# One core: an opening in which the norm of the first slot runs between two reaction pairs, and slot 0 has its own order

## The chip, the core and the metric

The kernel runs on one core of a Trainium2 chip. The metric is the device time of one execution in microseconds. The kernel before took 1431.0 us, the median of 3 runs (1430.63 to 1432.73). The engines are TensorE (PE), VectorE (DVE), ScalarE (ACT), GpSimd (POOL) and SyncE (SP), which here only issues transfers. Each has its own instruction queue, and they meet at semaphores alone.

## The reference

An input of 8 sequences of 256 tokens with 128 features runs through eight stages. The change touches the first two: a reaction-diffusion step, and four layers of a selective scan (Mamba). The later ones (an expert-routed feed-forward, a pooled attention, a quantized feed-forward) are unchanged. Cut to what matters:

```python
def cond(y, zX, zY, zR):                       # the "reaction"
    lap_x = y[.., :-2] - 2*y + y[.., 2:]       # along the features (reflected ends)
    lap_y = y[:-2] - 2*y + y[2:]               # along the tokens
    return zX*lap_x + zY*lap_y + zR*y*(1 - y)

for i in range(4):                             # layers
    x = x + mamba(layer_norm(x, ln_g, ln_b), ...)
# mamba: in-projection; causal convolution of 4 taps; silu; xdbl = x_proj(xm)
#   dt = softplus(dt_w @ xdbl[:8] + dt_b); B, C = the other 32 rows of xdbl
#   h[t] = exp(dt*A) * h[t-1] + dt*B*xm        # 16 states for each of 256 channels
#   y = sum_s h*C + xm*D_skip; y *= silu(z); out-projection
```

## The kernel before, in words

Features lie on the 128 partitions. The 8 sequences are taken in **pairs** (512 columns), and a pair in one layer is a **slot**: 16 slots, numbered by t; slot t handles pair t mod 4 in layer t div 4. In a slot the two sequences are called a and b. The scan over time runs in 8 chunks of 2 states for each sequence: chunk c of sequence a needs `dA:ac` (ScalarE, four exponentials into PSUM, L1198), `mul:ac` (the product of B and u, L1214 on VectorE or L1220 on GpSimd), `scan:ac` (VectorE, L1233), `C:ac` (product with C, GpSimd, L1239) and `sum:ac` (TensorE, L1268). `gate:a` (VectorE, L1277) follows the last sum.

While a slot scans, the engines prepare the next slot's front: `center` (TensorE L1060, x minus its mean), `square` (ScalarE L1064), `var` (TensorE L1068), `lnv` and `rstd` (ScalarE L1072, L1076), `norm` (VectorE L1080), `xn` (ScalarE L1085), `conv` (TensorE L1093, 16 matmuls), `xm` (L1100), `z` and `zs` (L1106, L1112), `xproj` (L1119), `xd` (L1126), `dt` (TensorE L1130, ScalarE L1144 to L1152, VectorE L1156) and `u` (L1164, half on VectorE and half on GpSimd). `ucopy` (ScalarE L1182) copies u into PSUM for VectorE's products. SP writes xd to memory (L995) and spreads its rows over all partitions: B0 and B1 (tile Bb), C0 and C1 (tile Cb), 2 MB each (L1001).

The order on each engine in a slot is a string of such names (`PE_ORDER`, `ACT_ORDER`, `DVE_ORDER`, `POOL_ORDER`), which `in_order` turns into code; a leading `l` means the previous slot's b, `n` the next slot's a, and `+` the slot after the next. Slot 0 and slot 13 are written out, slots 1 to 12 are a loop of two slots a pass, and slots 14 and 15 have orders of their own with the next stage woven in. In slot 0 the names of a previous slot are left out.

Ahead of slot 0 is the **opening**. TensorE turns the input (L1796, four turns of 4 transposes) and takes the laplacian along the features (L1803); ScalarE copies (L1831, L1838); GpSimd computes the product `rate(k)` of pair k (L1758) and, for each layer L, `bundle(L)`: one product of the in-projection with the taps (L1768) and two diagonal matrices (L1772). VectorE's `reaction(k)` has eight instructions (L1880 to L1890) and ends with pair k in `xs`. The bundles of layers 1 to 3 are stored in memory by SP (`store`, L975). The first convolution needs bundle 0 and the norm of pair 0, which needs `reaction(0)`. The first products overwrite what the reactions use, so they wait for all four reactions, and those of sequence b for the three stores.

Of the kernel before, what the change touches and what calls it, by code (L numbers as in the profile page):

```python
# [15 lines left out]
B, S, D = 8, 256, 128  # L16
# [70 lines left out]
def program(nc, io):  # L87
    with ExitStack() as ctx:
# [869 lines left out]
        def _(e):  # L958
# [65 lines left out]
            store(1)  # L1024
            e.wait_ge(sem("scr"), 16)
            raw(3)
            store(2)
            store(3)
            e.wait_ge(sem("scr"), 16 * (LAYERS - 1))
            for k, n in enumerate(("itok_B_0_7", "itok_B_0_2")):  # L1030
                e.dma_start(ids[:, k * B:(k + 1) * B], io[n].rearrange("(a b) -> a b", a=1)).then_inc(sem("ids_in"), 16)
            for t in range(SLOTS):
                L, r = divmod(t, NPAIR)
                if r == 1 and L:
                    load_out(L)
# [677 lines left out]
            for token in order.split():  # L1713
                piece(e, table, token, -1, 1)

        def slots(e, slot):

            slot(e, 0, 0, False, 2)
            with e.Fori(0, (SLOTS - 4) // 2) as j:
                slot(e, j * 2 + 1, 1, True, 2)  # L1720
                slot(e, j * 2 + 2, 0, True, 2)
            slot(e, SLOTS - 3, (SLOTS - 3) % 2, True, 2)
# [3 lines left out]
        def _(e):  # L1726
# [64 lines left out]
        @block.tensor  # L1791
        def _(e):

            def turn(k):
                for j in range(4):
                    m = e.transpose(bank(k)[:, j * P:(j + 1) * P], xtok[:, 4 * k + j, :], ident[:])  # L1796
                m.then_inc(sem("xT_ps"), 1)

            def lap(k):
                e.wait_ge(sem("xT"), TURNED[k])  # L1800
                if k > 1:
                    e.wait_ge(sem("xT"), TURNED[k - 2])
# [12 lines left out]
            first(e, PE, "center var")
            lap(2)
            lap(3)
            first(e, PE, "conv:0 conv:1 z:0 z:1 xproj dt:0 dt:1 +center +var")
            slots(e, in_order(PE, PE_ORDER))
            last(e, PE, FINAL_PE, PE_NEXT, LAST - 1)  # L1820
            last(e, PE, FINAL_PE, PE_LAST)
            tail_tensor(e)
# [4 lines left out]
        @block.scalar  # L1827
        def _(e):
            def turned(k):
                e.wait_ge(sem("xT_ps"), TURNED[k])  # L1830
                e.activation(ypad[:, 2 * k:2 * k + 2, 1:S + 1], bank(k).rearrange("p (b l) -> p b l", b=2),  # L1831
                             ACT.Copy).then_inc(sem("xT"), 1)

            def lap(k):
                e.wait_ge(sem("xT_ps"), LAPPED[k])
                e.wait_ge(sem("z_in"), 48)
                for b in range(2):
                    m = e.activation(lapx[:, 2 * k + b, :], bank((4 + k) % 6)[:, b * S:(b + 1) * S], ACT.Identity,  # L1838
                                     scale=zb[:, 0, 2 * k + b:2 * k + b + 1])
# [12 lines left out]
            e.wait_ge(sem("A"), 1)  # L1852
            e.activation(A_all[:], A_all[:], ACT.Copy, scale=-1.0).then_inc(sem("A"), 1)
            first(e, ACTE, "silus")
            lap(2)
            lap(3)
            e.wait_ge(sem("A"), 2)
            first(e, ACTE, "xm:0 xm:1 zs:0 zs:1 exps xd sp_abs sp_exp sp_ln ucopy:n dA:n0 dA:n1 +square +lnv +rstd")
            slots(e, in_order(ACTE, ACT_ORDER))
            last(e, ACTE, FINAL_ACT, ACT_NEXT, LAST - 1)  # L1860
            last(e, ACTE, FINAL_ACT, ACT_LAST)
            tail_scalar(e)
# [5 lines left out]
        def _(e):  # L1868
# [4 lines left out]
                ins.then_inc(sem("du"), 1)  # L1873
                e.wait_ge(sem("du"), count[0])

            def reaction(k):
                bb = slice(2 * k, 2 * k + 2)
                y, lx, ly, g = ypad[:, bb, 1:S + 1], lapx[:, bb, :], lapy[:, bb, :], grow[:, bb, :]
                e.wait_ge(sem("xT"), TURNED[k])
                du(e.tensor_copy(ypad[:, bb, 0:1], ypad[:, bb, 2:3]))  # L1880
                du(e.tensor_copy(ypad[:, bb, S + 1:S + 2], ypad[:, bb, S - 1:S]))
# [1 line left out]
                du(e.scalar_tensor_tensor(out=ly, in0=y, scalar=-2.0, in1=ly, op0=ALU.mult, op1=ALU.add))  # L1883
                e.wait_ge(sem("z_in"), 48)
                du(e.tensor_tensor(ly, ly, zb[:, 1, bb].unsqueeze(2).to_broadcast([P, 2, S]), ALU.mult))
                e.wait_ge(sem("rise"), k + 1)
                du(e.scalar_tensor_tensor(out=g, in0=y, scalar=-1.0, in1=rise[:, bb, :], op0=ALU.add, op1=ALU.mult))
                du(e.tensor_tensor(g, ly, g, ALU.subtract))
# [150 lines left out]
```

## Time and profile before

| | |
|---|---|
| median of 3 runs | 1431.0 us |
| profiled execution | 1420.1 us, span 1418.3 us |
| mean granted TensorE clock | 0.961 |
| busy: PE, DVE, ACT, POOL | 90%, 82%, 71%, 79% |
| first product of slot 0 (DVE L1214) | 50.61 us |
| first product of slot 1 | 106.34 us |
| first and last norm (L1080) among the slots | 58.03 and 774.05 us |

The norm that stands in slot t belongs to the front of slot t + 1; the norm of slot 0's own front is that in the opening, at 25.87 us. The shares are averages over a kernel with several stages: up to about 890 us the scan runs, and VectorE and GpSimd are the fullest engines; afterwards it is other work. All times in the rows are from the start of the span. A number in square brackets behind a row is the time in which the engine was idle before it, with what ended that.

### The profile page before, as it was taken

To read this page: it belongs to the slowest core of one execution; us is meant where nothing else is said; L and a number is where in the kernel's file an instruction comes from. 1 tells how busy PE (TensorE), PEld (TensorE's weight loads), DVE (VectorE), ACT (ScalarE), POOL (GpSimd) and SP (SyncE) were. 2 spreads that over 40 slices of the span, in tenths; PEclk is the share of its full clock that TensorE was granted. 3 is DMA by queue.
4 is the path that set the end of the run, shared out by engine and by line. 5 is a ranking of instruction groups with operands and counts; after the bars stand their busy time and mean duration, and the time that the engine had idled before them with its cause. 6 is when DMAs were issued, how large, how long until landed. Compare 5 with 4: busy or idle time off the path is not lost.

```text
span 1418.3 us, 19878 instructions
## 1 busy us (share of the span) xinstructions
PE 1273.4 (90%) x5370; PEld 708.4 (50%) x5379; DVE 1164.4 (82%) x1686; ACT 1010.6 (71%) x2389; POOL 1116.7 (79%) x684
## 2 busy tenths in 40 slices
PE   5689899898998999989989999879959999999994
PEld 2233443343443334334333355679945666766663
DVE  7599999999999999999999989755644576666664
ACT  3588788778878878878877887433326787887773
POOL 7499999999999999999999997044444777766662
PEclk8799999999999999999999999989978999999997
DMA  5541543443355254254345361413220000000000
GB/s 170 239 180 62 237 200 124 181 179 157 140 207 214 83 238 179 74 244 179 139 167 222 135 196 64 149 37 104 65 64 17 7 22 24 12 20 17 9 9 9
DMA packets 48978, 169.26 MB, mean 119 GB/s; under 512 B 15704, under 2 KB 33436, under 8 KB 40716
## 3 DMA queue, kind: packets, MB, share of 16 engines
q1 hardware_dynamic: 46636, 163.78, 30.1%
q0 software_dynamic: 2272, 4.66, 1.4%
q8 instruction: 31, 0.51, 0.1%
q14 instruction: 39, 0.32, 0.1%
HBM read 160.75 MB, written 7.67 MB: 119 GB/s over the span
## 4 chain that ended last, share of the span: by engine, by line
PE 46%; DVE 24%; ACT 14%; issue 11%; POOL 2%; DMA 2%; DVEq 0%; ACTq 0%; POOLq 0%; SPq 0%
DVE h L1233 13%; ACT banks L1198 10%; PE banks L1268 7%; DVE h L1214 5%; PE banks L403 5%; PE banks L728 3%; PE banks L789 3%; PE banks L766 3%; PE banks L412 2%; PE banks L670 2%; PE banks L685 2%; PE banks L1119 2%; PE banks L705 2%; PE banks L804 2%; PE banks L1285 2%
## 5 line engine op out<-in xcount | busy, mean ns | idle before, releaser
L1239 POOL TENSOR_TENSOR h<-h,Cb 128x1024 f32<-128x1024 f32 (+1 forms) x180 | 584.5, 3275 | 29.7 <-DVE h L1233 18.6
L1233 DVE TENSOR_TENSOR_SCAN h<-banks,h 128x1024 f32<-128x1024 f32 x256 | 573.9, 2278 | 15.7 <-ACT banks L1198 15.4
L1198 ACT ACTIVATE banks<-dt,A_cur 128x255 f32<-128x255 f32 x1024 | 422.4, 461 | 89.0 <-DVE h L1233 86.8
L1268 PE MATMUL banks<-h,ident 128*128 128x512 f32 x1024 | 468.9, 597 | 5.2 <-POOL h L1239 3.3
L1268 PEld LDWEIGHTS banks<-h,ident 128*128 128x128 f32 x1024 | 189.8, 190 | 248.8 <-issue 225.9
L1214 DVE TENSOR_TENSOR h<-Bb,banks 128x1024 f32<-128x1024 f32 (+1 forms) x131 | 204.7, 1568 | 2.9 <-ACT banks L1182 2.9
L1220 POOL TENSOR_TENSOR h<-Bb,u 128x1024 f32<-128x1024 f32 x80 | 188.6, 2369 | 0.3 <-DMA Bb<-scrX 0.3
L758 POOL TENSOR_SCALAR h<-h 128x128 f32<-128x128 f32 (+1 forms) x128 | 96.3, 768 | 59.5 <-DVE h L751 59.3
L758 POOL TENSOR_SCALAR Cb<-Cb,h 128x128 f32<-128x128 f32 (+1 forms) x128 | 102.6, 819 | 32.5 <-DVE h L751 32.4
L1093 PE MATMUL banks<-xn,wF 128*128 128x512 f32 x256 | 117.6, 612 | 8.8 <-ACT xn L1085 8.8
L1093 PEld LDWEIGHTS banks<-xn,wF 128*128 128x128 f32 x256 | 49.8, 196 | 75.1 <-issue 63.1
L403 PE MATMUL banks<-Cb 128*128 128x128 f32 x624 | 78.2, 280 | 0.0
L382 POOL COPY Bb<-Bb 128x1 int32 x39 | 10.5, 269 | 85.0 <-DVE Bb L1637 45.4
L403 PEld LDWEIGHTS banks<-Cb 128*128 128x128 f32 x624 | 75.0, 197 | 0.0
L737 DVE CUSTOM_DVE_ANT_0 h<-banks,Bb 128x128 f32<-128x128 f32 (+1 forms) x128 | 39.1, 352 | 30.0 <-PE banks L728 29.5
L728 PE MATMUL banks<-h 64*128 64x128 f32 (+1 forms) x512 | 59.3, 350 | 0.5 <-DVE h L737 0.4
L488 DVE TENSOR_TENSOR Cb<-Cb,banks 128x512 f32<-128x512 f32 x39 | 26.8, 688 | 37.9 <-PE banks L403 37.9
L745 ACT ACTIVATE h<-h 128x128 f32<-128x128 f32 (+1 forms) x128 | 56.7, 450 | 0.0
L745 ACT ACTIVATE Cb<-Cb,h 128x128 f32<-128x128 f32 (+1 forms) x128 | 56.5, 446 | 0.1
L789 PE MATMUL banks<-Bb,h 128*64 128x256 f32 (+1 forms) x512 | 55.8, 338 | 0.3 <-issue 0.3
L737 DVE CUSTOM_DVE_ANT_0 Cb<-banks,Bb 128x128 f32<-128x128 f32 (+1 forms) x128 | 39.2, 352 | 17.0 <-PE banks L728 16.2
L451 ACT ACTIVATE Cb<-banks 128x128 f32<-128x128 f32 x39 | 10.8, 278 | 56.2 <-PE banks L395 56.2
(295 smaller groups left out, 2047.3 us busy)
## 6 DMA issues: line engine op xcount, KB each, us to landing
Bb<-scrX SPq DMA_DIRECT2D x32, 2048.0 KB, 8.1
Cb<-scrX SPq DMA_DIRECT2D x32, 2048.0 KB, 9.6
h<-in_L_ffn_w SPq DMA_DIRECT2D x2, 2048.0 KB, 8.7
by_expert<-Cb SPq DMA_DIRECT2D x39, 64.0 KB, 1.5
h<-in_conv_w SPq DMA_DIRECT2D x4, 512.0 KB, 3.9
scr<-h SPq DMA_DIRECT2D x3, 640.0 KB, 3.0
wF<-scr SPq DMA_DIRECT2D x3, 512.0 KB
dt<-in_pmask SPq DMA_DIRECT2D x4, 257.0 KB, 2.7
```

Source lines behind the costliest of these rows:

```text
L403: m = e.matmul(bank(2 * w + q)[:, c * P:(c + 1) * P], w_now[q][w][:, c * P:(c + 1) * P], xgT[k], start=True, stop=True)
L728: m = e.matmul(bank(o)[:, lo:lo + n], qT[r:r + HS, p, jc * P:(jc + 1) * P], kT[r:r + HS, p, 0:n], start=True, stop=True)
L745: m = e.activation(Pr[h % 8][:, lo:lo + n], Pr[h % 8][:, lo:lo + n], ACT.Exp, bias=negm[:, jc, h:h + 1], scale=-1.0, accum_out=sums[:, jc, ...
L758: m = e.tensor_scalar(Pr[h % 8][:, lo:lo + n], Pr[h % 8][:, lo:lo + n], inv[:, jc, h:h + 1], None, ALU.mult)
L789: m = e.matmul(bank(4, S)[o * HS:(o + 1) * HS, q0:q0 + n], V[:, kc, h * HS:(h + 1) * HS], PT[h % 4][:, 2 * P * kc:2 * P * kc + n], start=( ...
L1093: m = e.matmul(ps_F[half][:].rearrange("p (b l) -> p b l", b=2), wF[:, FC_TAP + k * 2 * P + half * P:FC_TAP + k * 2 * P + (half + 1) * P], ...
L1198: m = e.activation(ps_dA[c % 2][:, g, half, 1:S], dts[q][:, half, i * S + 1:(i + 1) * S], ACT.Exp, scale=A_cur[q][:, s:s + 1])
L1214: e.tensor_tensor(h[i][:, rows(cs), :, :], both(Bb[i], cs), u_rows(ps_u, cs), ALU.mult).then_inc(sem("mulv"), len(cs))
L1220: e.tensor_tensor(h[i][:, rows(cs), :, :], both(Bb[i], cs), u_rows(us[q][:, :, i * S:(i + 1) * S], cs), ALU.mult).then_inc(sem("mulp"), le ...
L1233: e.tensor_tensor_scan(chunk(i, c), ps_dA_flat[c % 2], chunk(i, c), 0.0, ALU.mult, ALU.add).then_inc(sem("scan"), 1)
L1239: e.tensor_tensor(h[i][:, rows(cs), :, :], h[i][:, rows(cs), :, :], both(Cb[i], cs), ALU.mult).then_inc(sem("hC"), len(cs))
L1268: m = e.matmul(bank(5), ident[:], h_flat[i][:, s * HALVES * S:(s + 1) * HALVES * S], start=(s == 0), stop=(s == NS - 1))
```

## The change

Five edits. (1) In the opening GpSimd waits for `reaction(0)` before `bundle(0)`, and its order becomes rate 0, bundle 0, rate 1, bundle 1, rate 2, rate 3, bundle 2, bundle 3. (2) VectorE's reaction is cut in two: `across(k)`, the first five instructions, and `reaction(k)`, the last three; the norm now stands between `across(1)` and `reaction(1)`. (3) SP issues stores 2 and 3 after B0 and C0 of slot 0 instead of ahead of slot 0, and no longer waits there for the stores to land. (4) ScalarE and VectorE have an order of their own for slot 0 (`ACT_OPEN`, `DVE_OPEN`); GpSimd and TensorE keep theirs. (5) ahead of slot 0 ScalarE runs `+square` before `dA:n1` instead of after it.

```diff
@@ SP
             raw(3)
-            store(2)
-            store(3)
-            e.wait_ge(sem("scr"), 16 * (LAYERS - 1))
...
                 spread_B(t, 0)
                 spread_C(t, 0)
+                if t == 0:
+                    store(2)
+                    store(3)
                 spread_B(t, 1)
@@ every engine
-        def slots(e, slot):
-            slot(e, 0, 0, False, 2)
+        def slots(e, slot, opening):
+            opening(e, 0, 0, False, 2)
@@ GpSimd
             rate(0)
+            e.wait_ge(sem("res"), 1)
             bundle(0)
+            rate(1)
             bundle(1)
-            rate(1)
             rate(2)
+            rate(3)
             bundle(2)
-            rate(3)
             bundle(3)
@@ ScalarE
-            first(e, ACTE, "xm:0 ... ucopy:n dA:n0 dA:n1 +square +lnv +rstd")
+            first(e, ACTE, "xm:0 ... ucopy:n dA:n0 +square dA:n1 +lnv +rstd")
@@ VectorE
+            across(0)
             reaction(0)
-            reaction(1)
+            across(1)
             e.wait_ge(sem("ln_in"), 32)
             first(e, DVE, "norm")
-            reaction(2)
-            reaction(3)
+            reaction(1)
+            for k in (2, 3):
+                across(k)
+                reaction(k)
@@ the order of slot 0 on VectorE, first line
+mul:a0 scan:a0 mul:a12 scan:a1 norm scan:a2 mul:a4 scan:a3 scan:a4 gate:l mul:a6 scan:a5 scan:a6 mul:b0 scan:a7
```

VectorE in the opening. Before, the last three instructions of reaction 1 (L1887 to L1890) stand ahead of the norm (L1080):

```order
L1882 TENSOR_TENSOR h0<-ypad 128x512
L1883 SCALAR_TENSOR_TENSOR h0<-ypad,h0 128x512
L1885 TENSOR_TENSOR h0<-h0,zb 128x512
L1887 SCALAR_TENSOR_TENSOR h0<-ypad,h0 128x512
L1888 TENSOR_TENSOR h0<-h0 128x512
L1890 TENSOR_TENSOR xs<-h0 128x512
L1080 SCALAR_TENSOR_TENSOR xc<-banks,lng,rstd 128x512
```

and in the changed kernel, where they are L1892 to L1895:

```order
L1883 TENSOR_TENSOR h0<-ypad 128x512
L1884 SCALAR_TENSOR_TENSOR h0<-ypad,h0 128x512
L1886 TENSOR_TENSOR h0<-h0,zb 128x512
L1080 SCALAR_TENSOR_TENSOR xc<-banks,lng,rstd 128x512
L1892 SCALAR_TENSOR_TENSOR h0<-ypad,h0 128x512
L1893 TENSOR_TENSOR h0<-h0 128x512
L1895 TENSOR_TENSOR xs<-h0 128x512
```

The norm moved up past three instructions. VectorE at the start of slot 0, before (L1214 is a product, of two chunks where it is 2048 wide; L1233 a scan of one chunk):

```order
L1164 TENSOR_TENSOR u0<-dt0,xm0 128x512
L1214 TENSOR_TENSOR h0<-Bb0,banks 128x2048
L1080 SCALAR_TENSOR_TENSOR xc<-banks,lng,rstd 128x512
L1233 SCALAR_TENSOR_TENSOR h0<-banks,h0 128x1024
L1214 TENSOR_TENSOR h0<-Bb0,banks 128x1024
L1233 SCALAR_TENSOR_TENSOR h0<-banks,h0 128x1024 x2
```

and now:

```order
L1164 TENSOR_TENSOR u0<-dt0,xm0 128x512
L1214 TENSOR_TENSOR h0<-Bb0,banks 128x1024
L1233 SCALAR_TENSOR_TENSOR h0<-banks,h0 128x1024
L1214 TENSOR_TENSOR h0<-Bb0,banks 128x2048
L1233 SCALAR_TENSOR_TENSOR h0<-banks,h0 128x1024
L1080 SCALAR_TENSOR_TENSOR xc<-banks,lng,rstd 128x512
L1233 SCALAR_TENSOR_TENSOR h0<-banks,h0 128x1024
```

Two scans now stand ahead of the norm. ScalarE from the copy of u (L1182) ahead of slot 0, before (x4 of L1198 is one dA chunk):

```order
L1182 ACTIVATE banks<-u 128x512
L1188 ACTIVATE A_cur<-A_all 128x32
L1198 ACTIVATE banks<-dt,A_cur 128x255 x8
L1064 ACTIVATE rstd<-banks 128x512
L1072 ACTIVATE rstd<-banks,eps 128x512
L1076 ACTIVATE rstd<-rstd 128x512
L1085 ACTIVATE xn<-xc,lnb 128x2x256
L1198 ACTIVATE banks<-dt,A_cur 128x255 x12
L1134 ACT_TABLE_LOAD
L1100 ACTIVATE xm<-banks,wF 128x512 x2
```

and now:

```order
L1188 ACTIVATE A_cur<-A_all 128x32
L1198 ACTIVATE banks<-dt,A_cur 128x255 x4
L1064 ACTIVATE rstd<-banks 128x512
L1198 ACTIVATE banks<-dt,A_cur 128x255 x4
L1072 ACTIVATE rstd<-banks,eps 128x512
L1076 ACTIVATE rstd<-rstd 128x512
L1198 ACTIVATE banks<-dt,A_cur 128x255 x4
L1085 ACTIVATE xn<-xc,lnb 128x2x256
L1198 ACTIVATE banks<-dt,A_cur 128x255 x16
L1134 ACT_TABLE_LOAD
L1100 ACTIVATE xm<-banks,wF 128x512 x2
```

One dA chunk now stands behind the square, one ahead of xn, and four (a3 to a6) instead of three (a2 to a4) between xn and xm.

## Rows read from the trace of the kernel before

**Rows 1.** Busy time by stretch: start:end, length, each engine (instructions), PEclk, DMA share, GB/s

```profile
25.00:30.00 5.00, 2.58 (x3) 1.18 (x4) 4.90 (x6) 3.30 (x7) 5.00 (x5) 0.50 0.40 153
...
50.60:106.30 55.70, 43.81 (x89) 17.51 (x90) 49.81 (x27) 43.74 (x89) 45.08 (x16) 0.84 0.53 218
...
315.00:368.00 53.00, 49.22 (x113) 20.82 (x112) 51.15 (x29) 41.62 (x84) 50.78 (x18) 0.97 0.39 160
368.00:420.00 52.00, 48.30 (x115) 20.55 (x114) 51.65 (x30) 42.27 (x86) 51.54 (x19) 1.00 0.44 176
```

**Rows 2.** Timeline of DVE in the opening: start us, us, instruction, [idle before]

```profile
7.89 0.17 DVE L1880 COPY ypad<-ypad 128x2 f32<-128x2 f32 x1 [7.74 <-ACT ypad L1831]
...
11.19 2.72 DVE L1887 SCALAR_TENSOR_TENSOR h<-ypad,h 128x512 f32<-128x512 f32 x1
13.95 0.74 DVE L1888 TENSOR_TENSOR h<-h 128x512 f32<-128x512 f32 x1
...
25.87 0.74 DVE L1080 SCALAR_TENSOR_TENSOR xc<-banks,lng,rstd 128x512 f32<-128x512 f32 x1
...
34.21 0.16 DVE L1880 COPY ypad<-ypad 128x2 f32<-128x2 f32 x1
...
38.24 0.69 DVE L1890 TENSOR_TENSOR xs<-h 128x512 f32<-128x512 f32 x1
...
46.82 1.22 DVE L1156 SCALAR_TENSOR_TENSOR dt<-banks,sp 128x1024 f32<-128x1024 f32 x1 [7.81 <-ACT sp L1152]
```

**Rows 3.** Timeline of POOL in the opening

```profile
10.49 2.88 POOL L1768 TENSOR_TENSOR wF<-h 128x1024 f32<-128x1024 f32 x1 [1.53 <-DMA h<-in_skip]
13.35 1.81 POOL L1772 TENSOR_SCALAR wS<-ident,h 128x128 f32<-128x128 f32 x2
...
19.20 2.68 POOL L1758 TENSOR_TENSOR h<-ypad,zb 128x512 f32<-128x512 f32 x2
```

**Rows 4.** Timeline of PE in the opening, and the convolution of slot 1

```profile
13.72 0.78 PE L1796 MATMUL banks<-ident,h 128*128 128x128 f32 x4
15.52 1.12 PE L1060 MATMUL banks<-xs,center_w 128*128 128x512 f32 x2 [1.02 <-DVE xs L1890]
...
27.42 8.97 PE L1093 MATMUL banks<-xn,wF 128*128 128x512 f32 x16 [5.54 <-ACT xn L1085]
...
110.79 7.03 PE L1093 MATMUL banks<-xn,wF 128*128 128x512 f32 x16
```

**Rows 5.** Timeline of ACT in the opening

```profile
20.04 0.63 ACT L1076 ACTIVATE rstd<-rstd 128x512 f32<-128x512 f32 x1
```

**Rows 6.** Timeline of DVE at the start of slot 0

```profile
50.61 2.29 DVE L1214 TENSOR_TENSOR h<-Bb,banks 128x2048 f32<-128x2048 f32 x1 [1.84 <-ACT banks L1182]
58.03 0.75 DVE L1080 SCALAR_TENSOR_TENSOR xc<-banks,lng,rstd 128x512 f32<-128x512 f32 x1 [5.13 <-ACT rstd L1076]
58.69 2.28 DVE L1233 TENSOR_TENSOR_SCAN h<-banks,h 128x1024 f32<-128x1024 f32 x1
```

**Rows 7.** Timeline of ACT at the start of slot 0: two dA chunks

```profile
50.70 3.26 ACT L1198 ACTIVATE banks<-dt,A_cur 128x255 f32<-128x255 f32 x8
```

**Rows 8.** Timeline of POOL in slot 0: C:a01 and C:a2

```profile
64.42 6.84 POOL L1239 TENSOR_TENSOR h<-h,Cb 128x2048 f32<-128x2048 f32 x2 [7.23 <-DVE h L1233]
```

**Rows 9.** Transfers into Bb from 40 to 70 us: B0 is the shortest, B1 the longest

```profile
L1001 SPq DMA_DIRECT2D Bb<-scrX x2: 350/392/433, 43.2 to 44.0; - x2
...
DMA to landing us min/median/max: 6.9/11.5/16.2
```

**Rows 10.** Timeline of PE in the loop, the gap before L1283

```profile
327.96 1.97 PE L1283 MATMUL banks<-xs,ident 128*128 x2 [2.05 <-DVE yz L1277]
```

**Rows 11.** Timeline of DVE: three norms of the loop

```profile
313.17 0.75 DVE L1080 SCALAR_TENSOR_TENSOR xc<-banks,lng,rstd 128x512 f32<-128x512 f32 x1
365.67 0.74 DVE L1080 SCALAR_TENSOR_TENSOR xc<-banks,lng,rstd 128x512 f32<-128x512 f32 x1
416.36 0.75 DVE L1080 SCALAR_TENSOR_TENSOR xc<-banks,lng,rstd 128x512 f32<-128x512 f32 x1
```

More of the change, by code:

```diff
@@ L1775, in _ @@
             rate(0)
+            e.wait_ge(sem("res"), 1)
             bundle(0)
+            rate(1)
             bundle(1)
-            rate(1)
             rate(2)
+            rate(3)
             bundle(2)
-            rate(3)
             bundle(3)
             first(e, POOL, "u:0")
-            slots(e, in_order(POOL, POOL_ORDER))
+            slots(e, in_order(POOL, POOL_ORDER), in_order(POOL, POOL_ORDER))
             last(e, POOL, {}, POOL_NEXT, LAST - 1)
@@ L1818, in _ @@
             first(e, PE, "conv:0 conv:1 z:0 z:1 xproj dt:0 dt:1 +center +var")
-            slots(e, in_order(PE, PE_ORDER))
+            slots(e, in_order(PE, PE_ORDER), in_order(PE, PE_ORDER))
             last(e, PE, FINAL_PE, PE_NEXT, LAST - 1)
@@ L1857, in _ @@
             e.wait_ge(sem("A"), 2)
-            first(e, ACTE, "xm:0 xm:1 zs:0 zs:1 exps xd sp_abs sp_exp sp_ln ucopy:n dA:n0 dA:n1 +square +lnv +rstd")
-            slots(e, in_order(ACTE, ACT_ORDER))
+            first(e, ACTE, "xm:0 xm:1 zs:0 zs:1 exps xd sp_abs sp_exp sp_ln ucopy:n dA:n0 +square dA:n1 +lnv +rstd")
+            slots(e, in_order(ACTE, ACT_ORDER), in_order(ACTE, ACT_OPEN))
             last(e, ACTE, FINAL_ACT, ACT_NEXT, LAST - 1)
@@ L1874, in du, with across @@
                 e.wait_ge(sem("du"), count[0])
-            def reaction(k):
+            def across(k):
                 bb = slice(2 * k, 2 * k + 2)
-                y, lx, ly, g = ypad[:, bb, 1:S + 1], lapx[:, bb, :], lapy[:, bb, :], grow[:, bb, :]
+                y, ly = ypad[:, bb, 1:S + 1], lapy[:, bb, :]
                 e.wait_ge(sem("xT"), TURNED[k])
@@ L1885, in reaction @@
                 du(e.tensor_tensor(ly, ly, zb[:, 1, bb].unsqueeze(2).to_broadcast([P, 2, S]), ALU.mult))
+            def reaction(k):
+                bb = slice(2 * k, 2 * k + 2)
+                y, lx, ly, g = ypad[:, bb, 1:S + 1], lapx[:, bb, :], lapy[:, bb, :], grow[:, bb, :]
                 e.wait_ge(sem("rise"), k + 1)
@@ L1903, in _ @@
             first(e, DVE, "dt u:1")
-            slots(e, in_order(DVE, DVE_ORDER))
+            slots(e, in_order(DVE, DVE_ORDER), in_order(DVE, DVE_OPEN))
             r = Chain(e, "du", count[0])
@@ L1941 @@
 mul:a3 mul:a5 C:l7 mul:a7 C:a01 C:a2 mul:b3 C:a34 mul:b6 C:a56 C:a7 C:b0 C:b12 C:b3 u C:b4 C:b56"""
+ACT_OPEN = """
+dA:a2 xn dA:a3 dA:a4 dA:a5 dA:a6 silus xm:0 xm:1 exps ucopy:b dA:a7 dA:b0 silus zs:0 zs:1 exps dA:b1 xd dA:b2
+dA:b3 sp_abs sp_exp sp_ln dA:b4 dA:b5 +square dA:b6 dA:b7 +lnv +rstd ucopy:n dA:n0 dA:n1"""
+DVE_OPEN = """
+mul:a0 scan:a0 mul:a12 scan:a1 norm scan:a2 mul:a4 scan:a3 scan:a4 gate:l mul:a6 scan:a5 scan:a6 mul:b0 scan:a7
+mul:b12 scan:b0 scan:b1 scan:b2 mul:b45 scan:b3 mul:b7 dt gate:a scan:b4 scan:b5 scan:b6 scan:b7"""
 PE_NEXT = """
```

## The prediction, made before the changed kernel ran

> **What bounds the kernel now.** I read the busy time of stretches first, then the timelines of the opening engine by engine, then slot 0, then the starts of the norms in the loop. In the loop VectorE and GpSimd are full: in 368 to 420 us VectorE works 51.65 of 52 us and GpSimd 51.54 [rows 1]. What the change touches lies ahead of that. Slot 0 (50.6 to 106.3 us) has VectorE busy for 49.81 of 55.70 us, so 5.9 us are idle there, and 5.13 us of it stand in one place, ahead of the second norm [rows 1, 6]. Before slot 0 the path runs: first turn, reaction of pair 0 on VectorE, center and variance on TensorE, rstd on ScalarE, **norm** on VectorE, xn, 16 convolution matmuls, xm, z, xproj, xd, dt, u, first product at 50.61. Two things are slack on that path. rstd is ready at 20.67, but the norm starts at 25.87 because the reaction of pair 1 stands ahead of it in VectorE's queue [rows 2, 5]. And VectorE's short operations are stretched while GpSimd runs two-input products: L1887 takes 2.72 us beside the first bundle (10.49 to 13.37) where L1890, of the same shape and also with two inputs from SBUF, takes 0.69 once GpSimd is silent (38.24) [rows 2, 3]. The two alternate: each waits until the other's instruction is over.
>
> The whole stay of VectorE from 7.89 to 38.93 us is 31.0 us; the last reaction, run alone, takes 34.21 to 38.93, 4.72 us. Four of them and the norm are 19.6, so 11.4 us were waited. GpSimd's own two-input work is 4 bundles at about 2.2 (2.88 less the 0.69 that it waited itself) and 4 rates at about 0.65 (2.68 for two, half of it waiting), 11.4 us as well [rows 2, 3]. VectorE waits for all of it.
>
> **Part 1, bundles behind the first reaction.** Bundle 0 now starts after xs of pair 0. L1887 loses 2.03 us (2.72 to 0.69), so xs ends at 13.44 instead of 15.47. The rate ahead of it is unmoved. TensorE can use only part of that: its fourth turn runs 13.72 to 14.50, and center, which began at 15.52, can begin at 14.52 [rows 4]. Gain 1.00 us; rstd, which ended at 20.67 [rows 5], ends at 19.67.
>
> **Part 2, norm ahead of the rest of reaction 1.** After 13.44 VectorE has five instructions (across 1) before the norm. Alone they are 2 x 0.17 + 3 x 0.72 = 2.5 us, by the reaction that ran alone [rows 2]; bundle 0's product (2.2) and rate 1 (0.65, beside one of them) are waited for, which ends them at about 18.5. So rstd decides, the norm starts at 19.7, and the gain at the norm is 25.87 - 19.7 = 6.2 us. Bounds: 5.2 if TensorE gains nothing at center, 7.4 if rstd gains more than center does and VectorE's own 18.5 decides.
>
> **Part 3, the convolution's clock.** The 16 matmuls take 8.97 us here and 7.03 in slot 1 [rows 4]. The mean granted clock from 25 to 30 us was 0.50 (1.2 GHz) [rows 1], and TensorE had sat idle 5.54 us before the convolution. Its work ahead of that (the laps) ended at 21.9; now it ends near 20 and the convolution starts at 21.2, one or two us later. The saving lies between 0 and 1.94; I take 1.4, nearer the short gap. Parts 1 to 3: **7.6 us** at xd and dt, the conv-to-xd stretch being unchanged. B's transfer starts from xd and so moves with it: it landed 6.9 us after its issue, just before the first product [rows 9].
>
> **Part 4, what becomes late next.** Moving work behind the norm makes VectorE's reactions 1 to 3 the thing to watch, for dt (46.82 before, now wanted at 39.2) stands behind them. From 7.89: 18.9 us of reactions, 0.75 of norm, rate 0 (0.75), and the GpSimd products that fall on VectorE's work. Bundle 1's product runs mostly while VectorE waits for rstd (1.1 us) or norms from PSUM, which GpSimd does not hold up. The rest is 2.05 + 0.5 + 0.35 + 2 x 0.65 + 2 x 2.2 = 8.6. End: 7.89 + 18.9 + 0.75 + 0.75 + 8.6 + 1.1 = 38.0. That is 1.2 us ahead of dt. With every product on VectorE (11.4) it is 39.9, and the gain at dt falls to 6.9; at best the gain there is capped at 8.8. GpSimd ends its bundles near 33, far ahead of u. On SP, raw 2 and raw 3 follow bundle 0 and store 1 by some 2 to 3 us more than before, and have that time.
>
> **Part 5, stores 2 and 3 moved past B0 and C0.** They no longer stand between bundle 3 and scrX, whose xd now comes at about 33.4 us. They stand ahead of B1 and C1 instead: 1.28 MB at some 400 GB/s are 3.3 us. B1 landed 16.2 us after its issue at 44.0 [rows 9], T + 9.6 (T is the first product, 50.6 before); now T + 12.9. GpSimd's mul:b3, its first user, comes at T + 15.2 in part 6. Cost 0, with 2.3 us of cover; beyond it the cost would be what GpSimd cannot absorb.
>
> **Part 6, slot 0.** Before: product a01, then VectorE idle until rstd at T + 7.4, norm, scan a0 from T + 8.1 although its dA was ready at T + 1.8 [rows 6, 7]. Now, with 1.65 us for a dA chunk (half of 3.26), 2.2 for a scan, 1.1 and 2.2 for products: scan a0 1.8 to 4.0, product a12 to 6.2, scan a1 to 8.4, norm to 9.1, scan a2 to 11.3, product a4, scan a3 from 12.4, where before it began at T + 16.9: 4.5 us gained. ScalarE runs dA n0, square, dA n1 (to 4.0), lnv and rstd (to 5.9), dA a2, xn at 9.2. GpSimd's C:a01, which waited 7.23 us for scan a1, starts at 8.4 instead of 13.8, and with 6.84 us for it and C:a2 [rows 8] mul:b3 follows at 15.2. Then ScalarE takes part back. Its dA a3 to a6, table load, xm (not before the convolution ends, T + 19 to 20.4), table load and the copy of u run to 23.0, while VectorE wants that copy at 22.3: 0.7 idle. Then 0.5 before scan a7, 0.45 before b1 (behind zs), 0.75 before b2 (behind xd, itself behind xproj, which stands behind sum a3 on TensorE). VectorE's work in the slot is 49.9 us; idle 0.6 + 0.7 + 0.5 + 0.45 + 0.75 = 3.0 instead of 5.8. **Gain 2.8 us**. Bounds: 4.5 if ScalarE gives nothing back, 0 if xproj and xm come 3 us later (1.2 GHz held through the whole convolution).
>
> **Part 7, the loop.** VectorE is full there, so an earlier start is an earlier end; the tail follows its inputs. But the loop is not uniform. Norm to norm is 52.50 us, then 50.69 [rows 11], and the long slot has a mean clock of 0.97 against 1.00 [rows 1]: TensorE idles 2.05 us before L1283, waiting for the gate [rows 10], and in one slot of four the clock falls to 1.2 GHz after that gap, and 1.8 us are lost. Shifting the loop changes which slots those are; over the loop one more or one fewer: 0, with 1.8 either way.
>
> **Sum.** 7.6 + 2.8 + 0 = 10.4 us. The profiled execution took 1420.1 us with a span of 1418.3 and 1.8 around it; it would take 1409.7. The runs shown have a median of 1431.0, 10.9 above the profiled one, and I carry the difference over: **1420.6 us**.
>
> **The rivals.**
> A. *Only the front pays.* Slot 0 gives nothing: ScalarE's later xm and xd stall VectorE for all that was saved. For it: ScalarE already works 43.7 of the 55.7 us there. Against it: the stalls that I can place come to 3.0, not 5.8. 1431.0 - 7.6 = 1423.4.
> B. *The reactions bind dt.* GpSimd's one-input products (L1772, 0.7 to 0.9 us each) may block VectorE as well. Here L1888 ran in 0.74 us from 13.95 beside two of them (13.35 to 15.16) [rows 2, 3], which speaks against it. If the four of bundles 2 and 3 did block, 4 x 0.69 = 2.8 us, the reactions would end at 40.8, dt at 40.9, gain 5.9 + 2.8 = 8.7: 1422.3. If besides all of GpSimd's products fell on VectorE, 42.7: 1424.2.
> The Trainium skill ("SBUF — State Buffer", section "Who interferes with whom") has it that VectorE with two SBUF inputs and a GpSimd instruction that reads SBUF exclude each other for the whole instruction. The trace agrees for the two-input products (2.72 against 0.69), and not for the one-input ones; taken to the letter it is rival B.
> C. *Slower: the clock falls in every slot.* If the shift puts the loop where each gap before L1283 costs 1.8 us, 14 slots pay instead of 3 to 4, 10 more: 18 - 10.4 = +7.6, 1438.6. It decides from six more falls (6 x 1.8 = 10.8). Against it: a fall itself moves the loop by 1.8 us, and the slot after it is free of one [rows 11].
> D. *Nothing to be measured.* The stores push B1 late enough, or bundle 0 delays the weights: 1431. Against it: bundle 0's product is done at about 15.7, 5.5 us ahead of the convolution.
>
> **How the numbers follow.** Forecast 0.57, A 0.17, B 0.16, C 0.04, D 0.06. From no change a measurement of this kernel can tell about 0.2%, 2.9 us. Faster: forecast, A and B, 0.90; within: 0.06; slower: 0.04. The ends of the terms: 6.9 + 4.5 + 1.8 is 13.2 and with the cap 8.8 it is 15.1, down to 1415.9; 5.2 + 0 at the other end is 1425.8. Range 1416.0 to 1426.5, which holds A and B too.
>
> **What would show it.** L1887 of pair 0 at 0.7 us; the second engine row for center at about 14.5; norm at 19.7; ScalarE idle under 1 us before xn; convolution of 7 to 8 us; the reactions done by 38 to 39 and dt at about 39; the first product at 43.0. In slot 0 scan a0 starts 1.8 us after the first product, the idle ahead of the second norm is gone, and the product that opens slot 1 comes 52.9 us after slot 0's (55.7 before), at about 96. After that all is the same distance earlier to within 1.8. I am wrong if dt waits for VectorE's reactions, if the stalls behind ScalarE in slot 0 exceed 5 us, or if more than five loop slots take 52.5 us.

## The result, and the profile after

| | before | changed |
|---|---|---|
| median of 4 runs | 1430.8 us | 1418.8 us (1417.6 to 1420.6) |
| ratio | | 0.9915, interval 0.9898 to 0.9932 |
| profiled execution, span | 1420.1, 1418.3 us | 1419.8, 1417.9 us |

The changed kernel is 12.0 us faster; 10.4 had been forecast, in a range of 4.3 to 14.8 below 1430.8. Run again later it was 11.5 us faster (1407.3 against 1418.8, ratio 0.9918, 0.9898 to 0.9938). The two profiled spans differ by 0.4 us only, so they must be read stage by stage; why they say nothing as a whole stands at the end of this section.

**The opening.** Timeline of DVE in the changed kernel; it answers to [rows 2] and [rows 6]:

```profile
12.67 0.69 DVE L1895 TENSOR_TENSOR xs<-h 128x512 f32<-128x512 f32 x1
...
13.68 2.72 DVE L1883 TENSOR_TENSOR h<-ypad 128x512 f32<-128x512 f32 x1
16.44 0.74 DVE L1884 SCALAR_TENSOR_TENSOR h<-ypad,h 128x512 f32<-128x512 f32 x1
17.21 0.74 DVE L1886 TENSOR_TENSOR h<-h,zb 128x512 f32<-128x512 f32 x1
18.00 0.75 DVE L1080 SCALAR_TENSOR_TENSOR xc<-banks,lng,rstd 128x512 f32<-128x512 f32 x1
...
37.92 0.69 DVE L1895 TENSOR_TENSOR xs<-h 128x512 f32<-128x512 f32 x1
38.56 1.25 DVE L1156 SCALAR_TENSOR_TENSOR dt<-banks,sp 128x1024 f32<-128x1024 f32 x1
...
42.32 1.22 DVE L1214 TENSOR_TENSOR h<-Bb,banks 128x1024 f32<-128x1024 f32 x1 [1.79 <-ACT banks L1182]
44.17 2.29 DVE L1233 TENSOR_TENSOR_SCAN h<-banks,h 128x1024 f32<-128x1024 f32 x1 [0.63 <-ACT banks L1198]
...
50.95 0.73 DVE L1080 SCALAR_TENSOR_TENSOR xc<-banks,lng,rstd 128x512 f32<-128x512 f32 x1
...
94.50 2.26 DVE L1214 TENSOR_TENSOR h<-Bb,banks 128x2048 f32<-128x2048 f32 x1
```

Pair 0's xs is done at 13.36 us, and the 2.72 us instruction is now L1883, behind it: the clash with bundle 0 was moved, not removed. The norm starts at 18.0 instead of 25.87. Ahead of dt there is no idle time: VectorE goes straight from the last reaction (38.61) to dt, while ScalarE's sp had ended at 37.50, so dt is bound by the reactions. The first product comes at 42.32 instead of 50.61, **8.3 us** earlier. The product that opens slot 1 follows 52.18 us later instead of 55.73, another **3.55 us**. Together it is 11.84 us at slot 1 (94.50 against 106.34).

PE and ACT in the opening of the changed kernel, as in [rows 4] and [rows 5]:

```profile
13.63 1.02 PE L1060 MATMUL banks<-xs,center_w 128*128 128x512 f32 x2
15.34 1.12 PE L1068 MATMUL banks<-rstd,mean_w 128*128 128x512 f32 x2 [0.69 <-ACT rstd L1064]
...
19.57 7.14 PE L1093 MATMUL banks<-xn,wF 128*128 128x512 f32 x16 [1.38 <-ACT xn L1085]
```

```profile
17.22 0.63 ACT L1076 ACTIVATE rstd<-rstd 128x512 f32<-128x512 f32 x1
...
36.44 1.06 ACT L1152 ACTIVATE sp<-sp 128x1024 f32<-128x1024 f32 x1
```

Center starts 0.27 us after xs is there, the variance takes 1.12 us, at 2.4 GHz, and the whole convolution runs at 2.4 GHz too: 7.14 us instead of 8.97. The granted clock was 1.00 from 5 to 30 us.

**The loop.** Starts of the norms (DVE L1080) of slots 0, 1, 5, 9, 13 and 14, taken from the timelines: before 58.03, 108.52, 313.17, 517.84, 722.52, 774.05; changed 50.95, 96.68, 303.05, 507.72, 712.39, 763.92. The lead is 11.84 us at slot 1 and 10.13 at slot 14: of the loop's slots three last about 52.5 us before and four last 52.4 to 52.5 now, the others 50.7 to 50.8 in both. Behind the last norm it is the other way round: one clock fall of before is missing. In slot 14, 25.4 us after its norm, TensorE runs xproj for slot 15; first the row of before, then that of the changed kernel:

```profile
799.45 3.44 PE L1119 MATMUL banks<-xm,wF 128*40 128x512 f32 x4 [0.69 <-ACT zs L1112]
```

```profile
789.32 1.91 PE L1119 MATMUL banks<-xm,wF 128*40 128x512 f32 x4 [0.69 <-ACT zs L1112]
```

The granted clock over the 20 us that hold this xproj was 0.91 before and is 1.00 now. So where the next stage begins (the first L1448, at 875.58 and 863.94 us) the lead is 11.64 us again, and that is what the medians show.

**The tail.** From the last norm to the end of the span it is 644.3 us before and 654.0 now. The difference of 9.7 us lies in three of the eight attention sequences: one is 1.9 us longer, and two take 44.60 us instead of 40.88 (starts of L907: 1145.67, 1190.27, 1234.87, 1275.75). The end is another 1.9 us longer, and the missing fall takes 1.5 off. In each of the three sequences TensorE stands still for 1.7 to 2.0 us ahead of a matmul without a wait that the profile shows, and in two of them the granted clock then falls to 0.50:

```profile
1169.64 1.26 PE L789 MATMUL banks<-Bb,h 128*64 128x256 f32 x8 [2.02 <-issue]
```

The change did not cause this: the kernel before with one edit in the loop, the last run but one below, has it too. Four comparisons were made, and before itself stood at 1430.8, 1419.4, 1418.8 and 1429.1 us in them. In the traces of the changed kernel and of the four kernels of the fourth comparison three attention sequences are long (42.7 to 42.9 us with the stop alone, 44.4 to 44.6 with the clock's fall); in the traces of the second and third comparison none is. The profiled execution of before had none and took 1420.1, as in the second and third. So the changed kernel, traced at the high level, is set against a trace of before at the low one. At one level each, the gain is 12.0 and 11.5. The three later comparisons ran on a chip each, so whether the level belongs to the chip or to the moment is open.

### The profile page after: what moved, and what is told of

The parts are those of the page before. It is cut to its first block, busy times and chain, and to the rows that moved or that the text cites. A ratio compares the mean times of both kernels' runs of the same rounds, so it can differ in the third digit from the quotient of the medians.

```text
span 1417.9 us, 19876 instructions
## 1 busy us (share of the span) xinstructions
PE 1274.1 (90%) x5370; PEld 710.9 (50%) x5379; DVE 1161.4 (82%) x1686; ACT 1010.2 (71%) x2389; POOL 1116.0 (79%) x684
## 4 chain that ended last, share of the span: by engine, by line
PE 46%; DVE 23%; ACT 14%; issue 12%; DMA 2%; POOL 1%; DVEq 0%; ACTq 0%; SPq 0%; POOLq 0%
DVE h L1233 13%; ACT banks L1198 9%; PE banks L1268 7%; DVE h L1214 5%; PE banks L403 5%; PE banks L728 4%; PE banks L789 3%; PE banks L766 3%; PE banks L412 2%; PE banks L670 2%; PE banks L685 2%; PE banks L705 2%; PE banks L804 2%; PE banks L1285 2%; PE banks L1119 2%
## 5 line engine op out<-in xcount | busy, mean ns | idle before, releaser
L1239 POOL TENSOR_TENSOR h<-h,Cb 128x1024 f32<-128x1024 f32 (+1 forms) x180 | 584.8, 3276 | 25.9 <-DVE h L1233 15.5
L1233 DVE TENSOR_TENSOR_SCAN h<-banks,h 128x1024 f32<-128x1024 f32 x256 | 573.8, 2276 | 16.4 <-ACT banks L1198 16.1
L1198 ACT ACTIVATE banks<-dt,A_cur 128x255 f32<-128x255 f32 x1024 | 422.1, 461 | 86.9 <-DVE h L1233 84.7
L1214 DVE TENSOR_TENSOR h<-Bb,banks 128x1024 f32<-128x1024 f32 (+1 forms) x131 | 204.5, 1566 | 3.6 <-ACT banks L1182 3.6
L382 POOL COPY Bb<-Bb 128x1 int32 x39 | 10.4, 266 | 85.1 <-DVE Bb L1637 45.4
```

The costliest lines, as they stand in the source:

```text
L1198: m = e.activation(ps_dA[c % 2][:, g, half, 1:S], dts[q][:, half, i * S + 1:(i + 1) * S], ACT.Exp, scale=A_cur[q][:, s:s + 1])
L1214: e.tensor_tensor(h[i][:, rows(cs), :, :], both(Bb[i], cs), u_rows(ps_u, cs), ALU.mult).then_inc(sem("mulv"), len(cs))
L1233: e.tensor_tensor_scan(chunk(i, c), ps_dA_flat[c % 2], chunk(i, c), 0.0, ALU.mult, ALU.add).then_inc(sem("scan"), 1)
L1239: e.tensor_tensor(h[i][:, rows(cs), :, :], h[i][:, rows(cs), :, :], both(Cb[i], cs), ALU.mult).then_inc(sem("hC"), len(cs))
```

## The experiments

Times are medians, set against before in the same comparison, since its level differs. "T" is the start of the first product of slot 0 on VectorE, "T1" that of the product that opens slot 1.

**The opening alone.** Both orders of slot 0 and the square as before, the rest as changed:

```diff
-            slots(e, in_order(DVE, DVE_ORDER), in_order(DVE, DVE_OPEN))
+            slots(e, in_order(DVE, DVE_ORDER), in_order(DVE, DVE_ORDER))
```

> Opening, bundle wait and stores as in the changed kernel; slot 0 in the order of before. Theory 1 (two independent gains: 8.3 us up to the first product, 3.6 us in slot 0): first product at 42.3 us, slot 0 lasts 55.7 us as before (106.34 - 50.61), the product that opens slot 1 at 98.0, and the timed gain over before is about 8 us (ratio 0.994). Rival 2 (the two need each other: with the norm early, slot 0 without its own order gives part of the 8.3 back, or the own order alone carries the gain): slot 0 lasts over 57 us, gain under 5 us. Rival 3 (the timed 12 us are largely TensorE clock falls in the attention stage, 3.7 us each, that come or go with the phase): the rows up to slot 1 as in theory 1, but the timed gain off by 3.7 us or twice that from 8.

Measured: 1411.3 against 1419.4, ratio 0.9945 (0.9929 to 0.9962), 8.1 us faster. Its DVE timeline:

```profile
42.24 2.29 DVE L1214 TENSOR_TENSOR h<-Bb,banks 128x2048 f32<-128x2048 f32 x1 [1.84 <-ACT banks L1182]
49.66 0.75 DVE L1080 SCALAR_TENSOR_TENSOR xc<-banks,lng,rstd 128x512 f32<-128x512 f32 x1 [5.13 <-ACT rstd L1076]
...
97.90 2.26 DVE L1214 TENSOR_TENSOR h<-Bb,banks 128x2048 f32<-128x2048 f32 x1
```

T is 42.24, slot 0 lasts 55.66 with the old 5.13 us of idle time in it. That is theory 1, within 0.1 us. At the first L1448 the lead over before is 8.5 us.

**Slot 0's orders alone**, on the kernel before:

```diff
-            slots(e, in_order(DVE, DVE_ORDER))
+            slots(e, in_order(DVE, DVE_ORDER), in_order(DVE, DVE_OPEN))
```

and the same for ScalarE, with `dA:n0 +square dA:n1`.

> Opening as before; only the orders of slot 0 on ScalarE and VectorE and the square ahead of dA:n1. Theory 1: first product at 50.6, slot 0 lasts about 52.2 us, product that opens slot 1 at 102.8, timed gain 3.5 us. Rival 2: slot 0 shorter by under 1 us, since what it saves ahead of scan a0 is taken back by the late xn, xm and xd. Rival 3: rows as in theory 1, timed gain off by 3.7 us.

Measured: 1415.3 against 1419.4, ratio 0.9973 (0.9962 to 0.9984), 4.1 us faster. T is 50.16 and T1 102.34, so slot 0 lasts 52.18, as in the changed kernel. At the first L1448 the lead is 3.9 us. (T of before is 50.61 in its only trace; here and in another run below the same opening gives 50.16 and 50.21, so the 8.3 us of the opening are known to about 0.4.) The two parts are independent and add: 8.1 + 4.1 = 12.2, against 12.0 and 11.5 for both.

**No wait ahead of bundle 0:**

```diff
             rate(0)
-            e.wait_ge(sem("res"), 1)
             bundle(0)
```

> The changed kernel without GpSimd's wait for the first reaction. Theory 1 with the port as the reason for the wait: the first two-input instruction beside bundle 0's product again takes 2.7 us, xs of pair 0 ends at 15.4 instead of 13.4, norm at 20 to 20.7 instead of 18.0, first product 1.5 to 2.5 us later (the chain behind the norm slips by 2 to 2.7, of which 1.0 was slack against the reactions); timed 1.5 to 2.5 us slower than the changed kernel, 10 us faster than before. Rival: the wait is worth nothing, since it only moves the contention behind the first reaction and dt waits for the reactions anyway: first product within 0.5 us of 42.3.

Measured: 1411.3 against 1419.4 (0.9948, 0.9931 to 0.9965): 8.1 us under before, some 3.5 less than the changed kernel. Its DVE timeline:

```profile
10.49 2.72 DVE L1885 TENSOR_TENSOR h<-h,zb 128x512 f32<-128x512 f32 x1
...
14.80 1.41 DVE L1894 TENSOR_TENSOR xs<-h 128x512 f32<-128x512 f32 x1
...
22.64 0.75 DVE L1080 SCALAR_TENSOR_TENSOR xc<-banks,lng,rstd 128x512 f32<-128x512 f32 x1 [0.91 <-ACT rstd L1076]
...
41.76 1.23 DVE L1156 SCALAR_TENSOR_TENSOR dt<-banks,sp 128x1024 f32<-128x1024 f32 x1 [3.18 <-ACT sp L1152]
```

The clash with bundle 0's product is back, but its price had been put too low. In this order rate 1 follows bundle 0 at once and stretches xs as well, to 16.2. TensorE has then been idle for 2.77 us, and the granted clock is 0.50 from 16 to 20 us: center and variance take 2.08 us each instead of 1.02 and 1.12. The norm is 4.6 us later than in the changed kernel, T is 45.50, 3.2 later. dt now waits for ScalarE and not for the reactions.

**The norm behind reaction 1:**

```diff
             across(1)
+            reaction(1)
             e.wait_ge(sem("ln_in"), 32)
             first(e, DVE, "norm")
-            reaction(1)
```

> The changed kernel with the norm behind reaction 1 instead of ahead of its last three instructions. Theory 1: the norm starts at about 22 instead of 18.0 us, and of the 4 us 1.0 is slack against VectorE's reactions (dt waits for them in the changed kernel): first product 3 to 3.5 us later, 45.5, or 1 more if the convolution then begins at 1.2 GHz. Rival: dt is bound by the reactions and not by the norm: first product within 1 us of 42.3.

Measured: 1413.7 against 1419.4 (0.9963, 0.9949 to 0.9977). The norm starts at 23.14, T is 47.57, 5.3 later than in the changed kernel, and more than expected. Its PE timeline shows where the rest went:

```profile
24.69 8.71 PE L1093 MATMUL banks<-xn,wF 128*128 128x512 f32 x16 [5.82 <-ACT xn L1085]
```

TensorE idles 5.82 us before the convolution, as it did before the change (5.54), and pays for it: 8.71 us instead of 7.14. The early norm saves the wait and the clock. The sum: 5.1 us at the norm, less 1.0 of slack against the reactions, plus 1.6 of the convolution, is 5.7; the 0.4 us by which this exceeds the measured 5.3 are in the matmuls of dt, faster here (1.98 against 2.37).

**The stores ahead of slot 0 again**, with the wait for them:

```diff
             raw(3)
+            store(2)
+            store(3)
+            e.wait_ge(sem("scr"), 16 * (LAYERS - 1))
```

> The changed kernel with stores 2 and 3 back ahead of slot 0 and the wait for them. In the changed kernel bundle 3 ends at 34.4 us and xd at 31.8. Theory 1: SP issues store 3 at 34.5 and waits some 3 us for it, so xd goes to memory at about 37.5 instead of 31.9 and B0 lands 5.7 us later, at about 46; first product of GpSimd at 46 to 47 instead of 41.7, VectorE's by 3 to 4 us later than 42.3, and the timed median 3 to 4 us above the changed kernel's (ratio to before 0.994). Rival: the path to the first product is dt and u, not B0, so nothing is seen: within 1 us.

Measured: 1419.6 against 1429.1, ratio 0.9937 (0.9916 to 0.9957). SP, and then the first products on POOL and DVE, of this kernel:

```profile
29.29 6.42 SPq L975 DMA_DIRECT2D scr<-h  x2
38.35 0.54 SPq L1031 DMA_DIRECT2D ids<-in_itok_B  x2
38.93 0.34 SPq L995 DMA_DIRECT2D scrX<-xd  x1
40.57 0.35 SPq L1001 DMA_DIRECT2D Bb<-scrX  x1
```

```profile
48.18 2.35 POOL L1220 TENSOR_TENSOR h<-Bb,u 128x1024 f32<-128x1024 f32 x1 [6.58 <-DMA Bb<-scrX]
```

```profile
48.13 1.22 DVE L1214 TENSOR_TENSOR h<-Bb,banks 128x1024 f32<-128x1024 f32 x1 [7.66 <-DMA Bb<-scrX]
```

xd was written to memory at 38.9 instead of 31.9 and B0 issued at 40.57 instead of 33.49; both engines wait for it, T is 48.13, 5.8 us later. Without the moved stores the opening would have kept only 2.5 of its 8.3 us. The expected 3 to 4 us were too low: xd was written 1.4 us later than expected, and B0 was there 9.2 us behind it instead of 8.5. At the last norm only 2.0 us are left of it (765.77 against 763.82 in the next kernel), since this run's loop has two long slots and that one's four. By medians it keeps 9.6 us of gain where the next kernel, in the same comparison and otherwise like the changed one, has 15.5; the two intervals overlap, so the rows (5.8 us) are the better evidence.

**The square behind dA:n1 again:**

```diff
-"... ucopy:n dA:n0 +square dA:n1 +lnv +rstd"
+"... ucopy:n dA:n0 dA:n1 +square +lnv +rstd"
```

> The changed kernel with the square behind dA:n1 again, ahead of slot 0; the rest of slot 0's order stays. Theory 1 (the gain of slot 0 comes from the two scans ahead of the norm): rstd ends 1.6 us later, about 49.8, still ahead of the norm's turn at 50.9, so slot 0 lasts 52.2 as in the changed kernel and the time is its own, 11 to 12 us under before. Rival: the early square carries the gain: slot 0 longer by over 1 us.

Measured: 1413.6 against 1429.1, ratio 0.9913 (0.9882 to 0.9943). rstd ends at 49.74, the norm starts at 50.93 all the same, and T to T1 is 42.30 to 94.48, 52.18 us. The early square is worth nothing; what is left of the new orders, the two scans ahead of the norm with ScalarE's order for them, carries the gain of slot 0. The time is 15.5 us under before where 11 to 12 were expected; its interval, 8.1 to 16.9 us, holds both, and the last norm, at 763.82, is where the changed kernel has it.

**A pure delay ahead of dt:**

```diff
+            for _ in range(2):
+                du(e.memset(yz[:], 0.0))
             first(e, DVE, "dt u:1")
```

> The changed kernel with two fills of 1024 columns put ahead of dt on VectorE, 1 to 2 us of pure delay. Theory P: the first product comes later by that delay and slot 0 lasts as long, but the falls in the loop and in the attention stage come elsewhere: the total is not simply the changed kernel's plus the delay, and can be several us lower. Rival Q: the total is the changed kernel's plus the delay, 1 to 2 us slower, within 1 us.

and the changed kernel itself, unedited, in the same comparison:

> The changed kernel itself once more, on the chip of the runs beside it. Theory P (phase): up to slot 1 it is 11.8 us ahead of before on any chip (94.50 against 106.34), but how many clock falls of 3.7 us the attention stage has (none in the profiled execution of before, two in that of the changed kernel) depends on the phase in which the stage is entered, so the timed difference from before may be anything from 4 to 16 us, in steps of 3.7, and is the 12.0 of the first comparison only by chance. Rival Q (what is gained at slot 1 is gained in the end): 10 to 12 us faster than before on this chip too, as in the first comparison.

The changed kernel itself took 1407.3 against 1418.8, the delayed one 1410.8 (0.9941, 0.9922 to 0.9961). T is 44.58 against 42.26, 2.3 us of delay; the last norm comes at 764.46 against 763.82, only 0.6 us later, since its loop has one long slot fewer. But by the medians the total is 3.4 us longer, not 0.6. The profiled execution of the delayed kernel, at 1407.5, is 3.3 us under its own median, so its rows do not show where the rest went. Theory P thus holds for the loop, where the number of falls changes by one and 1.8 us with it. For the whole the runs speak against it: two comparisons give 12.0 and 11.5, and in the medians the delay of 2.3 us is not given back.

**Bundle 3 in slot 0**, behind GpSimd's third product, with store 3 between B1 and C1:

```diff
             bundle(2)
-            bundle(3)
             first(e, POOL, "u:0")
...
+                in_order(POOL, "mul:a3 mul:a5 mul:a7")(e, p, q, prev, nxt)
+                bundle(3)
```

> The changed kernel with bundle 3 taken out of the opening into slot 0, behind the third product on GpSimd, and store 3 between B1 and C1. Theory R (dt waits for the reactions, which wait 2.2 us for bundle 3's product): the last xs ends at 36.4 instead of 38.6, dt starts at the end of ScalarE's sp, 37.5 instead of 38.56, first product 1.0 us earlier at 41.3; in slot 0 GpSimd is some 1.4 us late at C:a01 and has caught up by the end, slot 0 lasts 52.2 as before. Rival: POOL's lateness in slot 0 reaches VectorE (a scan waiting for mul:b3 or b6, or the gate for C:a7), slot 0 lasts 1 us or more longer and nothing is gained at slot 1.

Measured: 1406.4 against the changed kernel's 1407.3 and before's 1418.8 (0.9907, 0.9887 to 0.9927). Its DVE timeline:

```profile
35.66 0.69 DVE L1901 TENSOR_TENSOR xs<-h 128x512 f32<-128x512 f32 x1
...
37.08 1.22 DVE L1157 SCALAR_TENSOR_TENSOR dt<-banks,sp 128x1024 f32<-128x1024 f32 x1 [0.66 <-ACT sp L1153]
```

The reactions end at 36.35, 2.3 us earlier, and dt waits for ScalarE again: that shows what had bound it. T is 40.82, 0.5 earlier than expected, since sp ended at 37.05 and not at 37.5, and the norm of slot 1 at 95.17, 1.44 us earlier than in the changed kernel; slot 0 is not longer. In the medians 0.9 us is too little to be told from nothing.

**z ahead of out in the loop.** In every slot of the loop TensorE waits 1.95 to 2.07 us for the gate, and in the long ones the clock falls behind that wait. z needs only xm, which is ready:

```diff
-conv:0 conv:1 sum:l6 sum:l7 out z:0 z:1 sum:a0 ...
+conv:0 conv:1 sum:l6 sum:l7 z:0 z:1 out sum:a0 ...
```

> The changed kernel with TensorE's z:0 z:1 ahead of out in the loop, so that they fill the 2 us in which TensorE idles before L1283. Theory F (that gap lets the clock fall once in four slots, at 1.8 us a time): no slot of 52.4 us is left in the loop, all are 50.7, the norm of slot 14 comes 5 to 7 us earlier than in the changed kernel (763.9), and the timed median falls by as much, apart from what the attention stage's phase adds. Rival G (the falls come from another gap, the one before center, or z ahead of out makes out and res late and stalls ScalarE): slots of 52.4 remain, or every slot grows by 0.2 us or more.

Measured: 1396.5 against the changed kernel's 1407.3 and before's 1418.8, ratio 0.9836 (0.9816 to 0.9856). The gap on PE in slot 1, in the changed kernel and then in this one:

```profile
111.48 1.74 PE L1283 MATMUL banks<-xs,ident 128*128 x2 [2.06 <-DVE yz L1277]
113.00 3.01 PE L1285 MATMUL banks<-yz,wS 128*128 128x512 f32 x4
```

```profile
109.06 1.88 PE L1106 MATMUL banks<-xn,wF 128*128 128x512 f32 x4
111.30 1.12 PE L1283 MATMUL banks<-xs,ident 128*128 x2 [0.36 <-DVE yz L1277]
112.25 1.88 PE L1285 MATMUL banks<-yz,wS 128*128 128x512 f32 x4
```

The gap shrinks from 2.06 to 0.36 us, the clock stays up, and every slot of the loop lasts 50.40 us: none is long, and the short ones are 0.3 to 0.4 us shorter too. The last norm is at 752.73 instead of 763.82. Expected were 5 to 7 us; it is 11.1 because the short slots gained too: four falls of 1.7 and 0.3 to 0.4 in every slot.

**The same on the kernel before:**

```diff
-conv:0 conv:1 sum:l6 sum:l7 out z:0 z:1 sum:a0 ...
+conv:0 conv:1 sum:l6 sum:l7 z:0 z:1 out sum:a0 ...
```

> The kernel before with z:0 z:1 ahead of out in the loop. Theory F (the gap before L1283 costs the loop the same with either opening): first product and slot 0 as before (50.6, 55.7), all loop slots 50.4, last norm at 774.05 less 11 = 763, timed gain 9 to 11 us (ratio 0.993). Rival (the gain belongs to the state in which the new opening leaves the loop): slots of 52.4 remain, or a gain under 5 us.

Measured: 1420.4 against 1429.1, ratio 0.9944 (0.9923 to 0.9964), 8.8 us, just under the 9 to 11 expected. T is 50.21, the loop slots are 50.4, the last norm 764.23 instead of 774.05. The edit has nothing to do with the opening.

**Both additions to the changed kernel**, the two edits above together:

```diff
-            bundle(3)
             first(e, POOL, "u:0")
...
-conv:0 conv:1 sum:l6 sum:l7 out z:0 z:1 sum:a0 ...
+conv:0 conv:1 sum:l6 sum:l7 z:0 z:1 out sum:a0 ...
```

> The changed kernel with bundle 3 in slot 0 and z ahead of out, both. Theory R and F add: first product 40.8, slot 0 as in the changed kernel, loop slots of 50.4, last norm at 751.3, timed 24 us under before (0.983). Rival: the attention stage, entered at another time, takes back 3.7 us or more.

Measured: 1403.5 against 1429.1, ratio 0.9835 (0.9802 to 0.9868), 25.6 us. T is 40.85, the last norm 751.40. This one and the version with z alone beat both kernels; between these two the measurements do not decide, and the rows give bundle 3's move 1.3 us.

## Why the prediction was right

The path was named rightly and the two parts are where they were put; the sum of 10.4 was 1.6 us short of the first comparison, 1.1 of the second. In the rows the terms are 8.3 (forecast 7.6), 3.55 (2.8), -1.7 for the loop (0) and +1.5 for slot 14 behind it (not forecast), 11.6 in all. That the last two nearly cancel is luck: at the last norm the lead was 10.1. Term by term:

- *Part 1, xs of pair 0 at 13.44.* Measured 13.36. Center was to start at 14.52, behind the fourth turn; it started at 13.63, because the turn was through earlier as well.
- *Part 2, norm at 19.7 by rstd.* **The mis-sized term.** rstd ended at 17.85 and the norm started at 18.0, bound by VectorE's own five instructions (17.95). The gain was 7.87 us and not 6.2, more than the bound of 7.4. That bound took VectorE's five to end at 18.5, and its own terms add up to 18.8; but rate 1 ran beside the norm, which it did not hold up, and not beside them. rstd was early because center came 0.9 us earlier than thought, and the variance took 1.12 us at 2.4 GHz, where before it took 1.95 in a stretch whose clock fell. I had carried the interval from center to rstd over unchanged. The run without the bundle wait shows the other side: there the clock falls, and the norm starts at 22.6.
- *Part 3, the clock of the convolution, 1.4 of at most 1.94.* Measured 1.83.
- *Part 4, the reactions as the next bound.* Forecast end 38.0, 1.2 us ahead of dt, with a cap of 8.8 us on the gain. They ended at 38.61, and because parts 2 and 3 gave more, they became the bound: dt could have started at 37.5. Of 9.3 us the cap let 8.2 through at dt. Taking bundle 3 away lifted it. "dt waits for VectorE's reactions" was one of the prediction's own signs of being wrong, and it came: the bound at dt was named wrongly, at a price of 1.1 us, while the number held.
- *Part 5, the stores at no cost.* B1 was there: GpSimd went from C:a2 to mul:b3 without a wait. What was not priced is what the move itself bought, 5.8 us; the sum held only because the edit was in it.
- *Part 6, slot 0, 2.8 us.* Measured 3.55, with and without the new opening. The idle times at T + 1.8 and ahead of b0 came as forecast (0.63 and 0.73), those ahead of a7 and b1 smaller (0.36, 0.30), and the 0.75 ahead of b2 did not come: xd followed its dA chunk without a wait, since xproj was through at 2.4 GHz.
- *Part 7, the loop, 0 with 1.8 either way.* One long slot more: -1.7. Slot 14, which no term covered, has one clock fall less: +1.5.
- *The difference of 10.9 us between profile and median*, carried over. It was no property of the kernel: the changed kernel's own profiled execution is 1.0 us above its median. It is a difference in level between comparisons, which goes with the stops in the attention stage, and carrying it over was right only because the result was measured beside before, at the same level. At the low level the changed kernel took 1407.3, where 1409.7 had been forecast for a profiled execution.

The rivals: A (only the front pays) falls with the orders run alone, 4.1 us. B (the reactions bind dt) came true in its mechanism but not its price, and not through the one-input products: L1884 ran in 0.74 us from 16.44 beside two of GpSimd's L1772 (15.83 to 17.65). Taken to the letter, the rule of the Trainium skill ("SBUF — State Buffer", section "Who interferes with whom") would have had it wait; here too the trace follows it for the two-input products (L1883, 2.72 us) and not for these. C fell: four long slots, not fourteen. D fell: the gain is clear of noise in both comparisons.

## What to carry to other kernels

When an operation moves up a queue, look at the clock of what follows: here a shorter wait on TensorE also meant matmuls at 2.4 GHz, in three places (variance and convolution by the opening, xproj by slot 0's orders: 1.91 us instead of 3.58). Before moving work out of the way, ask which queue it is moved past and who waits there; at the first product the stores' place on SP was worth more (5.8 us) than the orders of slot 0 (3.55). And a loop whose busiest engine is at 99% may still lose 1.8 us in three or four of its slots to an idle gap on another engine, which one swap of two independent operations removed.

## What the runs showed of the hardware

- An idle gap of 1.95 to 2.07 us on TensorE stood in every slot of the loop, and in three or four of them the granted clock fell to 0.5 behind it, which cost 1.7 to 1.8 us each. With the gap at 0.23 to 0.36 us no slot was long, and the short ones lost 0.3 to 0.4 us too. Over the loop that is worth 11 us here (9.8 on the kernel before), as much as the whole change.
- The clash of VectorE and GpSimd is moved by a reordering, not removed: 2.72 us for a 0.69 us instruction stands in L1887 before, in L1883 after and in L1885 without the wait. The norm, which reads PSUM, ran in 0.75 us beside rate 1. But VectorE's copies of 2 columns, with one input, were held up as well: before, the one at 15.39 us took 2.30 us beside bundle 1's product and 0.16 alone.
- A stop of 1.9 to 2.0 us on TensorE in the attention stage came in every trace taken in two comparisons and in none of the others, and goes with a level about 11 us higher for before and for the changed kernel. What causes it was not settled, nor whether it accounts for all of the 11 us: no timed run of before at the high level has a trace.
